# Layer norm's inverse root: from a ScalarE root and a VectorE reciprocal to twelve VectorE instructions

## What is computed

```python
def _layernorm(x, axis=-1, eps=1e-05):
    m = jnp.mean(x, axis=axis, keepdims=True)
    v = jnp.var(x, axis=axis, keepdims=True)
    return (x - m) / jnp.sqrt(v + eps)
```

## Time and profile before

| | |
|---|---|
| time, three runs | 2873.07, 2875.24, 2882.4 us (median 2875.24) |
| the profiled execution | 2872.0 us |
| its span, first to last instruction | 2870.2 us |
| mean granted TensorE clock | 0.947 of full speed |
| stages, L0 / A0 / L0 | 77 / 553 / 57 us |
| L1 / A1 / L1 | 222 / 779 / 224 us |
| L2 / A2 / L2 | 354 / 65 / 365 us |
| L3 / A3 / L3 | 71 / 25 / 78 us |

### The profile page before, as it was taken

The page is one execution under the profiler, slowest core; times in us unless marked ns, Lnnn a source line. Parts: engine busy times, 40 slices in busy tenths (PEclk is TensorE's granted clock), DMA queues, the critical chain, the costliest instruction groups (busy, mean ns, idle before and its releaser), DMA issues. The chain is left out here.

```text
span 2870.2 us, 39199 instructions
## 1 busy us (share of the span) xinstructions
PE 2580.3 (90%) x13384; PEld 1291.0 (45%) x13472; DVE 1636.7 (57%) x2746; ACT 1268.7 (44%) x2917; POOL 529.2 (18%) x571
## 2 busy tenths in 40 slices
PE   7989999987786799999999978869999879999988
PEld 3446666654784222222222237744444544444333
DVE  5778888854223888888888512233332432333454
ACT  3652333333453488878878855521110231111243
POOL 1235666611224300000000022210000000000112
PEclk9988999998897799999999988979999989999999
DMA  2343222202782320120200028941221012120222
GB/s 96 97 147 103 98 92 88 83 11 76 223 296 84 80 39 14 22 32 3 40 14 3 4 85 276 339 134 60 88 74 45 30 61 84 64 89 30 60 45 61
DMA packets 132359, 241.87 MB, mean 84 GB/s; under 512 B 17968, under 2 KB 84400, under 8 KB 129552
## 3 DMA queue, kind: packets, MB, share of 16 engines
q1 hardware_dynamic: 128104, 231.44, 26.6%
q0 software_dynamic: 4096, 8.40, 0.9%
HBM read 206.58 MB, written 32.89 MB: 83 GB/s over the span
## 5 line engine op out<-in xcount | busy, mean ns | idle before, releaser
L2655 DVE TENSOR_REDUCE big<-psum 128x2 f32<-128x1024 f32 x512 | 604.1, 1221 | 76.7 <-PE psum L2467 72.8
L2615 ACT ACTIVATE probs<-psum 128x512 f32<-128x512 f32 x1024 | 553.1, 600 | 138.4 <-PE psum L2488 127.0
L2488 PE MATMUL psum<-big,k_ops 128*128 128x512 bf16 x945 | 294.5, 386 | 11.8 <-ACT probs L2615 6.7
L1391 PE MATMUL psum<-big 128*128 128x512 f32 x512 | 233.1, 606 | 10.0 <-DVE big L1522 10.0
L2488 PEld LDWEIGHTS psum<-big,k_ops 128*128 128x128 bf16 x1024 | 81.2, 97 | 334.2 <-ACT probs L2615 262.6
L1416 PE MATMUL psum<-probs,big 128*128 128x512 f32 x512 | 222.0, 594 | 5.2 <-issue 3.6
L1405 PE MATMUL psum<-big 128*128 128x512 f32 x512 | 224.4, 594 | 0.0
L1733 POOL TENSOR_TENSOR big<-big 128x512 f32<-128x512 f32 x32 | 40.4, 1269 | 915.6 <-ACT big L1698 874.0
L1185 ACT ACTIVATE hidden<-psum,big 128x128 f32<-128x128 f32 x480 | 136.0, 371 | 159.1 <-PE psum L1100 109.1
L2467 PE MATMUL psum<-big,w_A_or_L_A 32*128 32x512 bf16 x1024 | 164.2, 398 | 25.6 <-DVE big L2655 13.9
L1238 DVE TENSOR_TENSOR probs<-psum,big 128x128 f32<-128x128 f32 x120 | 34.5, 291 | 265.1 <-PE psum L1108 169.3
(11 more groups left out here) (472 smaller groups left out, 3728.1 us busy)
## 6 DMA issues: line engine op xcount, KB each, us to landing
big<-in_experts SPq DMA_DIRECT2D x120, 578.0 KB
big<-row_store SPq DMA_DIRECT2D x96, 512.0 KB, 4.1
big<-step_rows SPq DMA_DIRECT2D x16, 1024.0 KB
qkv_chunks<-big SPq DMA_DIRECT2D x48, 256.0 KB, 2.3
big<-qkv_chunks SPq DMA_DIRECT2D x16, 768.0 KB, 4.6
big<-since_rows SPq DMA_DIRECT2D x32, 256.0 KB
big<-row_store SPq DMA_DIRECT2D x32, 256.0 KB, 5.1
slots<-slot_rows SPq DMA_DIRECT2D x24, 256.0 KB, 5.6
```

The lines of the kernel that those rows point to most:

```text
L1391: mm = pe.matmul(k.bank[4 + c % 2][:, :], w["gate"][:, e, c, :], scaled[:, e, :], start=(e == 0), stop=(e == E - 1))
L2488: pe.matmul(k.bank[2 + m % 3][:, :], k_ops[:, g % 2, h, kt * P:(kt + 1) * P], q_ops[:, g % 2, i % QB, h, :], start=True, stop=True).then_i ...
L2615: act.activation(probs[:, kt % 2, h, :], k.bank[2 + m % 3][:, :], ACT.Exp, scale=SCALE).then_inc(expd.sem, 1)
L2655: dve.tensor_reduce(into, k.row_pair[hp].rearrange("p (h t) -> p h t", h=2), AX.X, ALU.max).then_inc(row_max.sem, 1)
```

## The change

The root and the reciprocal are replaced by instructions on DVE alone. From the variance v (PSUM, plus eps into SBUF) the float's bits are shifted right by one and taken from 0x5f3759df (written as a product by -1 and a sum, on int32), which gives a first guess y of v to the power -1/2. Three Newton steps follow, y(1.5 - 0.5 v y y), each of three instructions. That is 12 instructions on 128x128 with 11 drains between them, since each reads what the one before has written. `ln_square`, which variance has used up by then, holds v and the intermediate value. `act_deviation` and its counter are gone everywhere, with the table set that the scan stage loaded ahead for it; DVE waits for `variance` itself. `dve_norm` waits for the counter of ACT's copy too (the root's counter had covered it before). No step of PE, POOL or the DMAs moves.

```diff
 AX = mybir.AxisListType
@@ -121,16 +122,14 @@
         self.centred = Later(k.counter(ln + "_centred"), later)
         self.squared = Later(k.counter(ln + "_squared"), later)
         self.variance = Later(k.counter(ln + "_variance"), later)
-        self.deviation = Later(k.counter(ln + "_deviation"), later)
         self.inverted = Later(k.counter(ln + "_inverted"), later)
         self.spread = Later(k.counter(ln + "_spread"), later)
         self.normed = Later(k.counter(ln + "_normed"), later)
-        self.copied = k.counter("ln_copied")
+        self.copied = Later(k.counter("ln_copied"), later)
 
     def passed(self):
-        if self.early:
-            self.k.passed({"ln_copied": NB})
-        self.k.passed({f"{self.ln}_{n}": NB for n in ("centred", "squared", "variance", "deviation", "inverted", "spread", "normed")})
+        self.k.passed({"ln_copied": NB})
+        self.k.passed({f"{self.ln}_{n}": NB for n in ("centred", "squared", "variance", "inverted", "spread", "normed")})
 
     def here(self, n):
         return self.xn[:, bass.ds(n * TB, TB)] if self.ring is None else self.ring[n % 2]
@@ -146,9 +145,7 @@
     def act_square(self, act, n):
         act.wait_ge(self.centred.sem, self.centred.at(n))
         act.activation(self.square[:, :], self.bank0[:, :], ACT.Square).then_inc(self.squared.sem, 1)
-        copy = act.activation(self.here(n), self.bank0[:, :], ACT.Copy)
-        if self.early:
-            copy.then_inc(self.copied.sem, 1)
+        act.activation(self.here(n), self.bank0[:, :], ACT.Copy).then_inc(self.copied.sem, 1)
 
     def pe_variance(self, pe, n):
 
@@ -160,14 +157,23 @@
                            start=True, stop=True)
         mm.then_inc(self.variance.sem, 1)
 
-    def act_deviation(self, act, n):
-        act.wait_ge(self.variance.sem, self.variance.at(n))
-        act.activation(self.sd[:, :], self.bank1[:, 0:P], ACT.Sqrt,
-                       bias=self.k.ln_eps[:, :]).then_inc(self.deviation.sem, 1)
-
     def dve_invert(self, dve, n):
-        dve.wait_ge(self.deviation.sem, self.deviation.at(n))
-        dve.reciprocal(self.sd[:, :], self.sd[:, :]).then_inc(self.inverted.sem, 1)
+
+        sd, var, step = self.sd[:, :], self.square[:, 0:P], self.square[:, P:2 * P]
+        dve.wait_ge(self.variance.sem, self.variance.at(n))
+        dve.tensor_scalar(var, self.bank1[:, 0:P], LN_EPS, None, ALU.add)
+        dve.drain()
+        dve.tensor_scalar(sd.bitcast(I32), var.bitcast(I32), 1, None, ALU.arith_shift_right)
+        dve.drain()
+        dve.tensor_scalar(sd.bitcast(I32), sd.bitcast(I32), -1.0, float(0x5f3759df), ALU.mult, ALU.add)
+        for i in range(3):
+            dve.drain()
+            dve.tensor_tensor(step, sd, sd, ALU.mult)
+            dve.drain()
+            dve.scalar_tensor_tensor(step, step, -0.5, var, ALU.mult, ALU.mult)
+            dve.drain()
+            last = dve.scalar_tensor_tensor(sd, step, 1.5, sd, ALU.add, ALU.mult)
+        last.then_inc(self.inverted.sem, 1)
 
     def pe_spread(self, pe, n):
 
@@ -179,6 +185,7 @@
 
     def dve_norm(self, dve, n, scale=None):
         dve.wait_ge(self.spread.sem, self.spread.at(n))
+        dve.wait_ge(self.copied.sem, self.copied.at(n))
         here = self.here(n)
         if scale is None:
             last = dve.tensor_tensor(here, self.bank1[:, :], here, ALU.mult)
```

The other hunks take the step out of ACT's orders. Five of them:

```diff
@@ -1161,8 +1164,6 @@
             def prepare(n, step):
                 if step == "centre":
                     norm.act_square(act, n)
-                elif step == "variance":
-                    norm.act_deviation(act, n)
                 elif step == "hidden":
                     act.wait_ge(r_pre.sem, r_pre.at(n))
                     act.activation(router_hidden[:, :], k.bank[1][:, :], ACT.Silu, bias=w["rb1"]).then_inc(r_hid.sem, 1)
...
@@ -1481,10 +1481,6 @@
                 elif ahead:
                     ahead.act(act, "square")
                 gate(n, 0)
-                if more:
-                    norm.act_deviation(act, n + 1)
-                elif ahead:
-                    ahead.act(act, "deviation")
                 gate(n, 1)
                 if more:
                     route.act_logits_out(act, n + 1)
...
@@ -1825,14 +1817,10 @@
         @block.scalar
         def _(act):
             act.activation(decay[:, :], w["a"], ACT.Tanh).then_inc(tanh_done.sem, 1)
-            act.preload_act_table_set("sqrt_and_others")
             norm.act_square(act, 3)
-            norm.act_deviation(act, 3)
             ahead.act(act, "square")
-            ahead.act(act, "deviation")
             ahead.act(act, "logits")
             ahead.second.act_square(act, 1)
-            ahead.second.act_deviation(act, 1)
             ahead.act(act, "exp")
             ahead.act(act, "rows")
 
...
@@ -2621,8 +2608,6 @@
 
                 norm.act_square(act, NB - 1)
                 for at in range(5 * NB):
-                    if at == 2:
-                        norm.act_deviation(act, NB - 1)
                     item(at // 5, at % 5)
                 max_rows_out(0)
                 for i in range(STEPS):
...
@@ -3390,8 +3374,6 @@
                     act.preload_act_table_set("sqrt_and_others")
                 if prev:
                     squares(c - 1)
-                    if not nxt:
-                        ahead.act(act, "deviation")
                     oT_copies(c - 1)
                 if not nxt:
                     ahead.act(act, "logits")
```

More of the change, by code:

```diff
@@ L14 @@
 BF16 = mybir.dt.bfloat16
+I32 = mybir.dt.int32
 ACT = mybir.ActivationFunctionType
@@ L613, in act @@
             self.norm.act_square(act, n)
-        elif step == "deviation":
-            self.norm.act_deviation(act, n)
         elif self.route is None:
@@ L865, in norm_step @@
                     norm.act_square(act, n)
-                elif step == 2:
-                    norm.act_deviation(act, n)
                 elif step == E - 1:
@@ L871, in norm_after @@
             def norm_after(step):
-                ahead.act(act, {0: 'square', 2: 'deviation'}.get(step))
+                ahead.act(act, {0: 'square'}.get(step))
             def route_after(step):
@@ L1192, in _ @@
             out_tokens(0)
-            for step in ("centre", "variance", "hidden", "tokens", "logits", "second"):
+            for step in ("centre", "hidden", "tokens", "logits", "second"):
                 prepare(1, step)
@@ L1202, in _ @@
                     if n + 2 < NB:
-                        prepare(n + 2, {0: "centre", 1: "variance", 5: "hidden", 6: "logits", 8: "tokens", 9: "second"}.get(m))
+                        prepare(n + 2, {0: "centre", 5: "hidden", 6: "logits", 8: "tokens", 9: "second"}.get(m))
                     if m in (1, 5, 9):
@@ L1208, in _ @@
                     if early and n > 1:
-                        next_norm(n - 2, {2: "square", 4: "deviation"}.get(m))
+                        next_norm(n - 2, {2: "square"}.get(m))
                     elif linear and n == NB - 1:
-                        next_norm(0, {0: "square", 2: "deviation", 6: "logits", 9: "exp", 11: "rows"}.get(m))
+                        next_norm(0, {0: "square", 6: "logits", 9: "exp", 11: "rows"}.get(m))
             if early:
                 next_norm(2, "square")
-                next_norm(2, "deviation")
         @block.vector
@@ L1506, in _ @@
                         down_prepare(n - 1, step)
-                        if n == NB - 1 and ahead and step == 0:
-                            ahead.second.act_deviation(act, 1)
                     for e in range(E):
@@ L1711, in _ @@
                     route.act_exp(act, routed(i, 0))
-                if normed(i, 1):
-                    norm.act_deviation(act, normed(i, 1))
                 if routed(i, 3):
@@ L1717, in _ @@
                 if ahead and n == NB - 2:
-                    ahead.act(act, ("square", "deviation", None, "square", "deviation")[c], c // 3)
+                    ahead.act(act, ("square", None, None, "square", None)[c], c // 3)
                 elif ahead and n == NB - 1:
-                    ahead.act(act, (None, "square", "deviation", None, None)[c], 2)
+                    ahead.act(act, (None, "square", None, None, None)[c], 2)
         @block.gpsimd
@@ L2635, in _ @@
                         if i == STEPS - 1 and ahead and m % GH == GH - 1:
-                            ahead.act(act, {0: "square", 2: "deviation", 6: "hidden", 8: "logits", 11: "exp", 14: "rows"}.get(m // GH))
+                            ahead.act(act, {0: "square", 6: "hidden", 8: "logits", 11: "exp", 14: "rows"}.get(m // GH))
                 copy_sums(STEPS - 1)
```

## The result

The changed kernel takes 2996.7 us in the median of six runs (2989.2 to 3001.9), the kernel before 2876.5 (six runs): a ratio of 1.042, 95% interval 1.0405 to 1.0432, so 120 us slower. The forecast was 2950 with a range of 2896 to 3000. The direction and the range held, the range by 3 us; of the loss, 77.5 us were forecast and 120 came. In the two profiled runs the difference is 126 us (2998.4 against 2872.0).

What follows compares the result with a forecast made beforehand. PE was taken as the bound, so only chain time that PE waits for counts. Exposed losses less gains, 66.0 us, plus 11.5 of stretch by POOL made 77.5 on 2872.0, so 2950 us, range 2896 to 3000.

Steps and rivals of the forecast that it cites:

- the rival that needed 1.5: Whole kernel faster, 2858 us, since ACT's load and root delayed PE; needs a chain under about 1.5 us; 4%.
- Rival 2: Whole kernel: no change, within 0.3%, as the chain fills DVE's idle time and later waits absorb late norms; 5%.
- rival 3: Whole kernel: small loss, 2884 to 2900 us, with drains nearly free and part of the delay caught up; 7%.
- Rival 4: Full exposure: all 44 norms pay 3.3 us each, 145 us, giving 3017 us; 12%.
- E: Seven norms of the second feed-forward stage, where PE waits for weights by DMA or a gather: cost 0.
- Rival 5: ACT's table loads fall by 38 and no more; changes the sum by 1.3 us at most; no chance given.
- D: Seven norms in the third feed-forward stage, bound by PE: 0.87 us late each, 6.1 us in all.
- F: Two gains, at the ends of the first two attentions: -1.6 and -2.5 us, together -4.1.
- Class C: Ten norms with two to four us of slack, where DVE had waited for the root: 14.2 us lost.
- G: Chain instructions stretched by POOL's products, in seven norms of the last feed-forward stages and one of L0: 11.5 us.
- A: Nine norms with no slack, in the first and second feed-forward stages and around the scan: 28.5 us lost.
- B: Nine norms with about one us of slack, in L0, A0's projection and the last feed-forward: 21.3 us lost.

Runs made afterwards that it cites:

- x4: Changed kernel, but at the second attention's start POOL waits for the last norm's inverse root before filling memory and splitting operands; 2990.1 us, ratio 1.0392.
- x11: Changed kernel, but the second attention's last norm keeps the old root on ScalarE and reciprocal on VectorE, POOL not held back; 2977.2 us, ratio 1.0343.
- x6: Changed kernel plus eight 128x128 products of constants on PE before the wait for the inverse root, at norms of three places; 2975.2 us, ratio 1.0352.
- x3: Changed kernel, but ScalarE still runs the root at its old place, on a constant into an unread tile, with its table loads; 3007.5 us, ratio 1.0453.
- x9: Kernel before, with the new chain for the last ten norms alone; 2913.0 us, ratio 1.0129.
- x10: Kernel before, with the full chain of three Newton steps at three norms alone; 2860.2 us, ratio 0.9940.

## Why the prediction was right, and where it was too small

**The price of the chain held.** 4.25 us from a row of another line against 4.19 measured; the bound without drains (3.3) and the rival that needed 1.5 are out. Rival 2 and rival 3 are out by the change itself. Rival 4 (145 us) is out as a whole, though the change came to within 25 us of it and its condition, that E is exposed too, holds at half of the norms of that stage. Rival 5 is out: the loads fell by 68 and not by 38. DVE is busy 1765.8 us and not some 1740; 11 of the 26 us between lie in the one chain that met the fill. PE's wait for the chain rose by 98 us and not by some 60.

**The range held by luck.** Its own working ended at 2990, which was moved to 3000 to take in more chance, and the measured 2996.7 lies between the two. The working had one stretch of 0.9 us for every norm above the sum, which is not what happened.

**D held, and F in its sum alone.** The third feed-forward stage, forecast 0.87 for each norm:

```profile
2053.45 0.43 PE L156 MATMUL psum<-ln_square,w_const 128*32 128x128 f32 x8
2053.95 0.29 DVE L164 TENSOR_SCALAR ln_square<-psum 128x128 f32<-128x128 f32 x1 [6.15 <-PE psum L156]
...
2058.20 1.05 PE L182 MATMUL psum<-ln_sd,w_const 128*128 128x128 f32 x7 [0.69 <-DVE ln_sd L175]
```

From the end of the variance (2053.88) to the spread 4.3 us, and the offset grows by 0.95 to 0.96 at five of the seven. At the end of the first attention:

```profile
619.29 0.43 PE L156 MATMUL psum<-ln_square,w_const 128*32 128x128 f32 x8
619.79 0.29 DVE L164 TENSOR_SCALAR ln_square<-psum 128x128 f32<-128x128 f32 x1 [2.66 <-PE psum L156]
...
624.70 1.64 PE L3208 MATMUL psum<-big 128*64 128x512 f32 x3 [3.00 <-DVE big L3465]
```

PE waits 3.0 instead of 4.69, 1.7 less, as worked out. At the second attention's end PE's 2.17 us are gone: from the end of the variance to the spread the trace has 4.3 us against 6.9, 2.6 gained. So both mechanisms are there. The sizes by the offsets are another matter: -3.6 at the first end, where -1.6 was forecast, and -0.03 at the second, where -2.5 was. That the two add up to nearly the forecast is luck; between these norms and the ones before lie 450 and 730 us of other work.

**The step that was too small is the one from chain to path**, at three places:

1. Class C, one norm: the prediction priced POOL's contention by a product with two inputs and said that one-input instructions show none, from the reciprocal. The chain has a one-input instruction on whole numbers, and POOL's next work at that place is a fill of 6.92 us, not a product of 1.27. I had not looked at what POOL does there. 12.8 us in place of 1.5; x4 and x11 show it. Elsewhere G was too large: 3.3 for the 9.9 of the last stages.
2. Class E, and two of C in the same stage: 0 for norms where PE later waits for transfers. The measured +20 for ten norms (forecast 6.5; 12.6 in the trace) says that this wait doesn't absorb the delay at all of them, but at half. The row that the reading rests on is a wait of DVE and not of PE. It also left out that PE's products after the stall free the buffers for the next weights; that this is the path is argued and not shown.
3. A, B and the last stages: I counted the stall itself, 3.3 at most, and a norm can cost 3.9 to 5.7, one in the last stage 8.1. Some 14 to 16 us of that is PE's clock after the stall, which the prediction named as unpriced, and in the last stages also DVE's own steps behind the chain and their meetings with POOL.

The three come to 11, 13 and 16 us in the changed kernel's trace, 40 of the 50 by which the table exceeds the forecast. Some 6 of the 13 are the L1 stage's own variation, and G's 6.6 lie on the other side, so that rather more than the 10 us left over has no cause shown.

## What stays open

The L1 stage varies by itself: between its first norm and its last, the offset grows by 16.5 us in the changed kernel's trace and by 9.5 to 11 in those of x4, x6 and x11, whose edits don't touch it, and of x3. One norm has 8.6 in the one and 0.3 to 0.8 in the others. That is some 6 us of the changed kernel's profiled 127, and it is why differences between single traces are read by stage here and not in all. Against the trace of before the same stretch takes 3.8 us less in x9, which has no chain there, and 4.2 less in x10, which has one. So a figure of one or two us at a single norm of this stage, or at the end of an attention, says nothing by itself.

## What to carry to other kernels

Before replacing one instruction on an engine that is "only 57% busy" by a chain, look at what the next engine in order does at the end of that chain: with the waiting engine in order, slack is a microsecond or two at each place and not the idle share, and beyond it a microsecond of chain can cost more than one. When instructions are added to VectorE, read at each place what GpSimd runs at that time, long memory fills above all. Making the change at three of 44 places alone, chosen from the traces, turned a loss of 4.2% into a gain of 0.6%, with all three steps; at two of them the traces show the old path late.

## What the runs showed of the hardware that was not expected

- A one-input `tensor_scalar` on int32 in SBUF (0.23 us alone) stood still for 6.88 us while GpSimd ran a memory fill of 6.92; one that reads PSUM ran in 0.28 us during such a fill.
- Eight useless products of 128x128 in each of the stalls of the first and the last stages made the kernel 19 to 21 us faster, of which 14 to 16 lie where they were added: the granted clock of the first stage stayed at 1.00 instead of 0.94.
- 102 us less work on ScalarE, 68 table loads among it, were worth about 10 us of time by the medians.
